# A selective scan with its rows on (state, 8 channels) instead of (channel) partitions

## The reference

```python
dA = jnp.exp(dtt[..., None] * A)
h = h * dA + (dtt * ut)[..., None] * bt[:, :, None, :]
y = jnp.einsum('bkdn,bkn->bkd', h, ct)
```

## Time and profile before

| | us |
|---|---|
| Median of 3 runs | 14557.88 (14551.72 to 14557.97) |
| The profiled execution | 14538.09 |
| its span | 14536.2 |
| busy: PE, DVE, ACT, POOL | 11496.1, 10145.5, 6001.9, 5066.4 |

### The profile page before, as it was taken

How to read it: one execution, slowest core, us unless ns; L and a number is a source line. 1 busy time by engine, 2 the same in 40 slices (tenths; PEclk the granted TensorE clock), 3 DMA queues, 4 the chain that set the end, 5 groups by cost and what they waited for, 6 DMA issues and landing times. The chain is left out here.

```text
span 14536.2 us, 114487 instructions
## 1 busy us (share of the span) xinstructions
PE 11496.1 (79%) x33392; PEld 4049.3 (28%) x33536; DVE 10145.5 (70%) x8934; ACT 6001.9 (41%) x6051; POOL 5066.4 (35%) x2435
## 2 busy tenths in 40 slices
PE   7778787787877878778787787878878788787877
PEld 2222322223222232222322223222232222322322
DVE  4957749577495775957759577595775957759586
ACT  3525335253352533525335253352533525335253
POOL 1614415144151441514415143151431514315143
PEclk8978879788797887978879788797887978779787
DMA  1000000000000000000000000000000000000000
GB/s 34 0 16 5 0 20 0 16 5 0 20 0 16 5 0 20 0 16 5 0 20 0 16 5 0 20 0 16 5 0 20 0 16 4 0 20 0 16 4 3
DMA packets 83051, 124.19 MB, mean 9 GB/s; under 512 B 31505, under 2 KB 32921, under 8 KB 82559
## 3 DMA queue, kind: packets, MB, share of 16 engines
q1 hardware_dynamic: 78111, 117.18, 3.2%
q10 hardware_dynamic: 3440, 1.10, 0.1%
q0 software_dynamic: 1104, 0.86, 0.0%
HBM read 18.36 MB, written 12.58 MB: 2 GB/s over the span
## 5 line engine op out<-in xcount | busy, mean ns | idle before, releaser
L1025 POOL TENSOR_TENSOR arena<-arena 128x1024 f32<-128x1024 f32 x1536 | 3646.5, 2374 | 1830.6 <-ACT arena L881 857.3
L777 PE MATMUL ps<-arena,c_ident 128*128 128x512 f32 x6144 | 3037.1, 617 | 862.4 <-POOL arena L1025 862.4
L966 DVE TENSOR_TENSOR_SCAN arena<-arena,ps 128x1024 f32<-128x1024 f32 x1536 | 3512.9, 2287 | 53.3
L881 ACT ACTIVATE arena<-ps 128x1024 f32<-128x1024 f32 x1536 | 1571.7, 1023 | 2100.8 <-POOL arena L1025 1929.8
L768 PE MATMUL ps<-arena,c_sel 96*128 96x512 bf16 x6144 | 1623.3, 386 | 429.4 <-ACT arena L881 162.8
L961 DVE TENSOR_TENSOR ps<-arena,ps 128x1024 f32<-128x1024 f32 x1536 | 1856.4, 1209 | 15.2 <-DVE arena L974 9.1
L876 ACT ACTIVATE arena<-arena,v_na 128x1024 f32<-128x1024 f32 x1536 | 1757.4, 1144 | 60.4 <-DVE arena L966 41.0
L777 PEld LDWEIGHTS ps<-arena,c_ident 128*128 128x128 f32 x6144 | 1048.4, 189 | 2359.0 <-POOL arena L1025 1600.1
L591 DVE TENSOR_REDUCE arena<-ps 128x1 bf16<-128x1024 f32 x768 | 933.6, 1223 | 995.2 <-PE ps L454 994.7
L1015 POOL TENSOR_TENSOR arena<-arena,XN 128x1024 f32<-128x1024 f32 x32 | 103.8, 3266 | 3324.9 <-DVE arena L956 3324.9
L571 ACT ACTIVATE arena<-ps 128x1024 f32<-128x1024 f32 x768 | 744.3, 1021 | 1036.4 <-PE ps L506 1036.4
(11 more groups left out here) (224 smaller groups left out, 12850.8 us busy)
## 6 DMA issues: line engine op xcount, KB each, us to landing
arena<-arena SPq DMA_DIRECT2D x1152, 64.0 KB, 2.0
arena<-arena SPq DMA_DIRECT2D x384, 32.0 KB, 2.0
XI<-in_x SPq DMA_DIRECT2D x17, 512.0 KB, 3.7
out_x<-X SPq DMA_DIRECT2D x16, 512.0 KB, 2.7
XI<-in_x SPq DMA_DIRECT2D x17, 256.0 KB, 4.2
out_x<-X SPq DMA_DIRECT2D x16, 256.0 KB, 3.3
arena<-in_sel_n SPq DMA_DIRECT2D x1, 2304.0 KB
w_o<-in_wo POOLq DMA_DIRECT2D x3, 96.0 KB, 10.0
```

Source lines behind the costliest of these rows:

```text
L777: mm = nc.tensor.matmul(ps[3][:, HALF * h:HALF * h + HALF], c_ident[:], hc[:, e, HALF * h:HALF * h + HALF], start=False, stop=stop, skip_g ...
L881: nc.scalar.activation(Cs[:, e, :], ps[2][:], ACT.Copy).then_inc(m_cc[g], 1)
L966: nc.vector.tensor_tensor_scan(hs[:, e, o], dA[:, e, o], ps[e][:, o], 0.0, ALU.mult, ALU.add).then_inc(m_h[g], 1)
L1025: pool.tensor_tensor(hc[:, e, :], hs[:, e, :], Cs[:, e, :], ALU.mult).then_inc(m_hc[g], 1)
```

## The change

A scanned tile now has partition p = 8 * state + channel: 16 states of 8 neighbouring channels of one direction. A step is one such block of channels; STEPS lists the 96 in four groups (direction pair s, channel tile c), each with its steps ordered by r, direction, q.

- dt and dt*u of all six tiles are stored to DRAM (scan_dt, scan_dtu), also the rows of B and C (scan_bc). For each step SyncE loads the 8 rows of dt and of dt*u, 16 copies of each, into 128 partitions (rings of three buffers, dtr and dur). B and C, each row copied to 8 partitions, are loaded once for each direction and stay in SBUF; ScalarE also copies the B blocks of the two directions in work to ps[0] and ps[1].
- ScalarE writes the decay into ps[2], one buffer. VectorE multiplies dt*u by B for two steps of three; GpSimd does it for the third, ahead of its own product with C.
- TensorE sums over the states with a matrix sel_y of 32 columns, into a quarter q of ps[3], in batches of four steps; the products wait in a ring of six. The identity sums, the spreading matmuls, the copies of C and the three-part cuts are gone.
- Sums are taken out of ps[3] by VectorE (taken), with D * u in the same instruction. The projection of attention and the input are written to partitions 64 to 127 as well, so that the normalised image has its last 64 channels twice.
- The preparation makes two projections of 76 rows, one for two directions, instead of four of 102; dt's six tiles go through clamp, Exp, Ln and a maximum that takes the bias from PSUM. Inner loops are written out.

The core of the diff, with the lines that the prediction speaks of:

```diff
@@ the steps @@
+        for g, (s, c) in enumerate(((0, 0), (0, 1), (1, 0), (1, 1))):
+            for r in range(4):
+                for k in (s, s + 2):
+                    for q in range(4 if c == 0 else 2):
+                        STEPS.append((g, k, 16 * c + 4 * q + r, q, r))
+        BATCH = 4
+        def on_pool(i):
+            return i % 3 == 2
@@ def scan_pe(pe) @@
+            for n in range(NSTEP // BATCH):
+                pe.wait_ge(m_hc, BATCH * (n + 1))
...
+                        mm = nc.tensor.matmul(ps[3][32 * q:32 * q + 32, HALF * h:HALF * h + HALF], sel_y[:, r, :],
+                                              hc[i % NHC][:, HALF * h:HALF * h + HALF], start=q not in fresh,
@@ def scan_sp(sp, b) @@
+                        sp.dma_start(dt_d[b, s + 2 * v, 0:128, :], DT[:, u, :]).then_inc(m_w[s], 16)
...
+                            sp.dma_start(du_d[b, s + 2 * i, 128:C, :], DU[64 * i:64 * i + 64, u, :]).then_inc(m_w[s], 16)
...
+                if i >= RING:
+                    sp.wait_ge(m_da, i - RING + 1)
+                sp.dma_start(dtr[:, i % RING, :], dt_d[b, k, 8 * j:8 * j + 8, :].unsqueeze(0).to_broadcast(
+                    [N, 8, L])).then_inc(m_dtl[i % RING], 16)
+                if i >= RING:
+                    wait_input(sp, i - RING)
+                sp.dma_start(dur[:, i % RING, :], du_d[b, k, 8 * j:8 * j + 8, :].unsqueeze(0).to_broadcast(
+                    [N, 8, L])).then_inc(m_dul[i % RING], 16)
@@ def scan_act(act) @@
-                nc.scalar.activation(dA[:, e, :], DT[:, t, :], ACT.Exp, scale=scale).then_inc(m_da[g], 1)
-                nc.scalar.activation(Cs[:, e, :], ps[2][:], ACT.Copy).then_inc(m_cc[g], 1)
+                act.wait_ge(m_dtl[i % RING], 16 * (i // RING + 1))
+                if i:
+                    act.wait_ge(m_h, i)
+                nc.scalar.activation(ps[2][:], dtr[:, i % RING, :], ACT.Exp,
+                                     scale=v_na[:, 24 * k + j:24 * k + j + 1]).then_inc(m_da, 1)
@@ def scan_dve(dve) @@
-                nc.vector.tensor_tensor(ps[e][:], DU[:, t, :], ps[e][:], ALU.mult).then_inc(m_bu[g], 1)
-                nc.vector.tensor_tensor_scan(hs[:, e, o], dA[:, e, o], ps[e][:, o], 0.0, ALU.mult,
+                if not on_pool(i):
+                    dve.wait_ge(m_dul[i % RING], 16 * (i // RING + 1))
+                    nc.vector.tensor_tensor(bu[:, i % 2, :], dur[:, i % RING, :], ps[k // 2][:], ALU.mult).then_inc(m_buv, 1)
+                wait_input(dve, i)
+                dve.wait_ge(m_da, i + 1)
+                if i >= 2:
+                    dve.wait_ge(m_hc, i - 1)
+                nc.vector.tensor_tensor_scan(hs[:, i % 2, o], ps[2][:, o], bu[:, i % 2, o], 0.0, ALU.mult,
@@ def scan_pool(pool) @@
+            def state_input(i):
+                pool.tensor_tensor(bu[:, i % 2, :], dur[:, i % RING, :], Bb[:, k, :], ALU.mult).then_inc(m_bup, 1)
+            for i in range(NSTEP):
+                if i + 1 < NSTEP and on_pool(i + 1):
+                    state_input(i + 1)
+                if i >= NHC:
+                    pool.wait_ge(m_y, (i - NHC) // BATCH + 1)
+                pool.tensor_tensor(hc[i % NHC], hs[:, i % 2, :], Cb[:, k, :], ALU.mult).then_inc(m_hc, 1)
```

More of the change, by code:

```diff
@@ L52, in consts @@
     group[:64, 1, :C] = same[128:]
-    row = np.arange(96)[:, None, None] % 32
-    blk = np.arange(48)[None, :, None]
-    half = np.arange(128)[None, None, :] // 64
-    sel_n = np.where(blk < 32, row == blk, row == blk - 32 + 16 * half).astype(np.float32)
+    group[:, :, C:] = group[:, :, 128:C]
+    sel_y = (np.arange(128)[:, None, None] % 8 + 8 * np.arange(4)[None, :, None]
+             == np.arange(32)[None, None, :]).astype(np.float32)
     h = np.arange(NH)
@@ L193, in two @@
                 loads.append((dst[0:64, 1], src[128:192]))
-            loads += [(c_ident[:], ident), (c_group[:], group), (c_ones[:], ones), (sel_f[0:96, :], sel_n),
+            loads += [(c_ident[:], ident), (c_group[:], group), (c_ones[:], ones), (sel_y[:], sel_y_),
                       (c_upper[:], upper), (c_heads[:], head_blocks), (selhead_f[0:STACK, :], sel_head),
@@ new lines, in inputs_by_pool, with inputs_by_vector, wait_input, source @@
+        def inputs_by_pool(i):
+            return sum(on_pool(j) for j in range(i + 1))
+        def inputs_by_vector(i):
+            return i + 1 - inputs_by_pool(i)
+        def wait_input(eng, i):
+            if on_pool(i):
+                eng.wait_ge(m_bup, inputs_by_pool(i))
+            else:
+                eng.wait_ge(m_buv, inputs_by_vector(i))
+        DT_PS = (2, 3, 0, 1, 2, 3)
+        def source(u):
+            s, v = u // 3, u % 3
+            return (XN, XT)[s][:, 0 if v < 2 else 1, :]
@@ L819, in scan_pe @@
                 for h in range(2):
-                    pe.wait_ge(ready, 2 + each * h)
+                    pe.wait_ge(ready, 4 if src is YA else 2 + each * h)
                     for c, m in enumerate(CT):
@@ new lines, in clamp, with softplus @@
+            def clamp(u):
+                dve.wait_ge(m_dtp, u + 1)
+                nc.vector.tensor_scalar(DT[:, u, :], ps[DT_PS[u]][:], v_dtb[:, u:u + 1], SOFTPLUS_LINEAR, ALU.add,
+                                        ALU.min).then_inc(m_cl, 1)
+            def softplus(u):
+                dve.wait_ge(m_ln, u + 1)
+                nc.vector.scalar_tensor_tensor(DT[:, u, :], ps[DT_PS[u]][:], v_dtb[:, u:u + 1], DT[:, u, :], ALU.add,
+                                               ALU.max).then_inc(m_dt, 1)
@@ new lines, in times_u @@
+            def times_u(u):
+                dve.wait_ge(m_dt, u + 1)
+                nc.vector.tensor_tensor(DU[:, u, :], DT[:, u, :], source(u), ALU.mult).then_inc(m_dud, 1)
+            for u in range(4):
+                clamp(u)
+            softplus(0)
+            clamp(4)
+            softplus(1)
+            clamp(5)
+            times_u(1)
+            softplus(2)
+            softplus(3)
+            dve.wait_ge(m_t, 2)
+            times_u(3)
+            softplus(4)
+            softplus(5)
@@ new lines, in scan_dve, with taken @@
+            times_u(5)
+            def taken(g):
+                last = GROUP_END[g] // BATCH + 1
+                dve.wait_ge(m_y, last)
+                c = g % 2
+                n = CT[c]
+                if g < 2:
+                    nc.vector.scalar_tensor_tensor(YA[0:n, c, :], XN[0:n, c, :], v_dsum[0:n, c:c + 1], ps[3][0:n, :],
+                                                   ALU.mult, ALU.add).then_inc(m_ev, 1)
+                else:
+                    dve.wait_ge(m_ev, g - 1)
+                    y = YA[0:n, c, :].rearrange("p (h w) -> p h w", w=W)
+                    nc.vector.tensor_tensor(y, y, ps[3][0:n, :].rearrange("p (w h) -> p h w", h=H),
+                                            ALU.add).then_inc(m_ev, 1)
```

510 lines of the change are left out of this document (202 added, 308 removed).

## The result

The changed kernel took 15308.8 us (median of four runs, 15270.6 to 15328.9) against 14557.6 us before: a ratio of 1.051, 95% interval 1.049 to 1.053. The forecast was 14508 us, slightly faster. The time lies inside the range that was given, and on the side of Rival 1: the transfers set the pace, at a rate between the two for which that rival was worked out. The profiled execution had a span of 15313.2 us, against 14536.2 before.

What follows compares the result with a forecast made beforehand. VectorE's 3.45 us a step was taken to bound the scan loop. Per image -9.8 (preparation) + 3.5 (loop) + 3.2 (behind it) = -3.1 us, times 16 -50: 14538.1 to 14488, plus 19.8 to the median, 14508 us; range 14290 to 16900.

Steps and rivals of the forecast that it cites:

- Rival 1: Scan loop: the transfers set the pace, at 213 GB/s 4.92 us a step, 16870 us in all; chance 35 in 100.
- Will the transfers keep up?: Scan loop: each step's loads, 1.049 MB at 426 GB/s, take 2.46 us and are covered by the step of 3.54.
- the prediction's own sign of being wrong: Loads of the scan loop: the forecast is wrong if the load of a block takes over 1.77 us.
- The bound of 296 GB/s: Scan loop: the rate below which the loads, 1.049 MB a step, are no longer covered by the 3.54 us step.
- Its lower case, 280 GB/s: Scan loop: with half the overlap of the DMA engines, 3.75 us a step, 27 us per image more, 14990 us.
- the single case put first: Whole kernel: transfers covered, slightly faster at 14508 us, own range 14290 to 14810; chance 55 in 100.
- Rival 2: Scan loop: matmuls on different column groups don't overlap, TensorE holds GpSimd, 5.3 us a step, 17100 us; chance 4 in 100.
- The loop without the transfers: Scan loop paced by scan and exponential in turn: 3.54 us a step, 339.8 us for 96 steps, 3.5 more than now.
- The handovers: Scan loop: passing from scan to exponential and back, 0.04 us each, within a pass of 3.51 us.
- those 9.8 us: Scan loop: loading the second set of B and C at 213 GB/s, 9.8 us, a term of Rival 1.
- The preparation: From the normalised input to the first scan: first scan 75 us behind L327's end, 9.8 us earlier than now.
- The tail: Behind the last scan: last product, last 16 matmul records and the taking, 11.7 us for 8.5 now, +3.2.

Runs made afterwards that it cites:

- e2: The changed kernel, but each load of the loop takes 128 different rows, one for each partition, instead of 16 copies of 8 rows: 14466.8 us.
- e7: The changed kernel, but each spread load writes 8 blocks of 16 partitions, each one row repeated, instead of 16 blocks of 8 adjacent rows: 16985.1 us.

## Why the prediction was wrong, step by step

**The step that failed is "Will the transfers keep up?"** The forecast took 426 GB/s from the earlier trace rows, a store of plain rows, for loads in 16 blocks of 8 partitions. The loads move 252 GB/s on average at a full share, 269 in the window above, where a block of 524 KB takes 1.95 us; the prediction's own sign of being wrong stood at 1.77. The bound of 296 GB/s follows from the step of 3.54 us, and well founded was the reason given for doubt: Rival 1 named the 16 blocks of 8 and the engines 32 partitions apart. Its lower case, 280 GB/s, gave 3.75 us a step and 14990 us; the loop has 3.89 in the window (11.68 / 3) and 400.7 / 96 = 4.17 on average. What was wrong is the weight. The store of 64 partitions at the half rate was in the rows, the new load had a shape that no row had, and the sum leant on the one number that made it come out faster. The chances as a whole stood at 57 in 100 for slower, but the single case put first had 55 on a question that the trace could not decide, and its sign was the wrong one. The shape is not all of the gap, either: the plain loads of e2, whose loop doesn't need more, moved 286 GB/s at a share of 0.81 over the loops, 355 for engines busy all the time and not 426.

One sum of a rival is off as well: 5.3 us a step and +165 us per image (Rival 2) make about 17,200 us, not 17,100. No conclusion hangs on it, since that rival took no part.

**The loop without the transfers**: forecast 339.8 us, e2 352.5. The chain of scan and exponential is right in kind, and e2's scans stand 3.6 us apart. Two terms were mis-sized. The handovers were taken at 0.04 each and are 0.10 and 0.08: 3.59 and not 3.51. GpSimd's step is 3.70. So (2 x 3.59 + 3.70) / 3 = 3.63, 348 us. The rest is the change from the first pair of directions to the second, where SyncE's queue brings four blocks of B and C ahead of dt: a gap of 6.7 to 7.8 us between two scans in e2, 10 to 12 in the changed kernel. I had counted those 9.8 us in Rival 1 alone, and they are on the path in either case. The exponential into PSUM, 1.118 us, lay within the bounds of 1.0 to 1.2.

**The preparation** was right: 76.3 us from the end of L351 to the first scan (1213.11 to 1289.42) where the sum had 75.6 and the kernel before has 85.4. Its end was in other hands than I had them: the last store was issued by 1271.4, and from there to the exponential at 1285.96 B, C and the first dt took 14.6 us, where I had 6.9 for loads and landing; the stores before them were as much earlier.

**The tail** was forecast at 11.7 us and is 8.8:

```profile
1686.64 2.29 DVE L945 TENSOR_TENSOR_SCAN arena<-ps,arena 128x1024 f32<-128x1024 f32 x1 [1.41 <-ACT ps L866]
...
1689.06 2.34 POOL L996 TENSOR_TENSOR arena<-arena 128x1024 f32<-128x1024 f32 x1 [0.33 <-issue]
...
1691.46 5.02 PE L784 MATMUL ps<-arena,sel_y 128*32 128x512 f32 x16 [6.82 <-POOL arena L996]
...
1696.53 1.21 DVE L929 TENSOR_TENSOR arena<-arena,ps 64x1024 f32<-64x1024 f32 x1 [7.60 <-PE ps L784]
1697.80 8.50 PE L794 MATMUL ps<-arena,c_mean 128*128 128x512 f32 x16 [1.32 <-DVE arena L929]
```

The 16 records on 32 columns took 5.02 us and not 7.8; in the loop, with four column groups and a granted clock of 0.50, they take 3.64. The reading of L522, that matmuls on different column groups overlap, held, and with it the answer to Rival 2.

**What the forecast had no term for** stands in the last row. The mean and the variance behind the scan are 16 records of full width. Before, they took 16.10 us (timeline and windows of the kernel before):

```profile
1586.41 16.10 PE L822 MATMUL ps<-arena,c_mean 128*128 128x512 f32 x16 [4.09 <-DVE arena L987]
```

```profile
1582.00:1586.40 4.40, 0.32 (x1) 0.00 (x0) 1.90 (x1) 2.04 (x2) 4.34 (x3) 0.97 0.00 0
1586.40:1590.00 3.60, 3.59 (x4) 1.00 (x4) 0.00 (x0) 0.00 (x0) 2.98 (x9) 0.50 0.00 0
```

and now they take 8.50 us. TensorE had stood idle for 4.1 us ahead of them, and the granted clock was 0.50, the lower of its two levels (1.2 GHz); now its last sums end 1.3 us ahead of them, after 5 us of work, and the granted clock is 0.92 and then 1.00, the upper one:

```profile
1693.90:1696.50 2.60, 2.58 (x12) 0.52 (x8) 0.00 (x0) 0.00 (x0) 0.00 (x0) 0.92 0.00 0
...
1700.00:1704.00 4.00, 4.00 (x8) 1.09 (x8) 2.55 (x4) 2.37 (x4) 3.01 (x9) 1.00 0.00 0
```

This gives 7.6 us an image, nearly as much as the shorter preparation. With it the account for this image is whole: -9.1 + 0.3 - 7.6 = -16.4 between two loops, and the scan rows gave -16.5 as the mean of all. It also corrects how e2's time is to be read: e2 came within 0.3% of the 14508 forecast, but because errors cancel: the loop 12.7 us too long; on the other side these 7.6 us, a preparation 1 us and a tail 2 us shorter than forecast, and 3.6 us in other stages that I haven't traced (548.7 us between its loops). That the sum was right but for the transfers would be too much to say.

## What to carry to other kernels

Before a stage is put on DMA, price the load in the very shape that it will have: how many blocks the outermost dimension makes, how many adjacent partitions each fills; 426 GB/s, from a store of plain rows, was 1.7 times what the loads moved over the loops (252), and where no row has the shape, the forecast is open and should say so. When a page says that an engine ended a wait, look at what that engine itself waited for. A window of 20 us can hit the one odd stretch of a run, as e7's did: hold its rate against the length of the whole loop before building on it. When a wait is added or an instruction moved in a queue, follow what stands behind it: two experiments here went wrong by 2600 and 290 us through one ScalarE copy.
